# Attention scores of the grouped-query layer: four 32-row tiles of TensorE in place of a zero-padded key matrix, with the softmax's steps dealt out anew to the engines

## The chip, the cores and the metric

The kernel runs on one core of one Trainium2 chip, in float32. The time is the device time of one execution in microseconds (us); lower is better. Engines are called PE (TensorE), DVE (VectorE), ACT (ScalarE), POOL (GpSimd) and SP (SyncE).

## The reference, cut to what matters

Four layers follow one another: a cross-attention block with a mixture of experts, a second attention with a choice of the best tokens, a grouped-query transformer layer, and a last attention. The change lies in the third. Its batch is 16, its sequences are 128 long, its width is D = 256; it has 16 query heads on 4 key heads, of head size 64.

```
NH, NKV, HD = 16, 4, 64
q, k = rope(q), rope(k)              # halves of 32: x1*cos - x2*sin, x2*cos + x1*sin
scores = einsum('bhqd,bhkd->bhqk', q, k) / sqrt(HD) + attention_mask
probs  = softmax(scores)             # over the 128 keys
attn   = einsum('bhqk,bhkd->bhqd', probs, v)
```

After it come the output projection, an RMS norm and a gated MLP of width 1024.

## The kernel before

The layer runs as a loop over G = 4 groups of GB = 4 batches. Within a group every engine has one queue of instructions, written out by hand, and semaphores tie the queues together: nothing overtakes within a queue.

In each group PE first projects keys and queries, DVE multiplies them with the cosine and sine tables (L1737), and POOL adds or subtracts the products to make the rotated halves `kr` and `qr` (L1712). A partition of these holds one of 4 key heads times one of 32 places within a half. Query heads are laid out as `a` (0 to 3, the place within a key head's four) by key head `i`.

For the scores the kernel before makes `kM2`: for each key head a copy of the keys in which the rows of the other three heads are zero (ACT, 8 instructions a group, L1677). One product over all 128 rows with 512 columns then gives, for one `a`, the scores of all 4 key heads at once (L1582, two halves added up). In the trace a float32 product is two MATMUL instructions, so that such a tile of scores is 4 rows of L1582.

A "tile" n = 4*j + t here is a [128 queries, 4 heads, 128 keys] block of batch j. 16 tiles make a group. It passes through:

1. PE: scores into bank `S[n % 4]` (semaphore `scored`).
2. DVE: scale and add the mask into SBUF (L1751, `masked`), then the maximum over the keys, negated (L1756, `maxed`).
3. ACT: four exponentials of 128 columns, each with its own bias and its own accumulated sum (L457, `probs`).
4. DVE: reciprocal of the sums (L1760, `divided`).
5. POOL: multiply the tile by it (`pool_scale`, L449, `scaled`).
6. PE: turn the four [128, 128] blocks into bank `T[n % 2]` (`pe_turn`, L467, `turned`). It waits for the copy of tile n - 2.
7. ACT: copy the turned tile to SBUF (L1689, `pt_ok`), in its queue `COPY_LAG` = 5 tiles behind the exponentials: the copy of tile m stands behind the exponential of tile m + 5.
8. PE: for each batch the products with the values (L1593); ACT copies them out (L1670).

PE has each tile's scores one batch ahead of the masks: `pe.wait_ge(M["masked"], n + 1)`, then the scores of tile n + 4, then the turn of tile n - 1 (`TURN_LAG` = 1).

Of the kernel before, what the change touches and what calls it, by code (L numbers as in the profile page):

```python
# [13 lines left out]
ALU = mybir.AluOpType  # L14
# [47 lines left out]
def build(nc, A, out):  # L62
    with ExitStack() as ctx:
# [65 lines left out]
        def view(at, shape):  # L129
            n = int(np.prod(shape))  # L130
            assert at + n <= W, (at, n)
            v = reg[:, at:at + n]
            if len(shape) == 1:
                return v
            names = "abcdefgh"[:len(shape)]
            return v.rearrange(f"p ({' '.join(names)}) -> p {' '.join(names)}",
                               **{k: s for k, s in zip(names[:-1], shape)})
# [49 lines left out]
        wu2 = view(l2w + 7168, [C, FF])  # L187
        wd2 = view(l2w + 9216, [FC, D])
        qr = view(12288, [GB, 2, NT])
        kr = view(0, [2, NT])  # L190
        kM2 = view(16384, [NKV, 2, NT])
        xn2 = view(16384, [GB, D])
        V2 = view(20480, [GB, NKV, HD])
        o2T = view(0, [FC, NT])
# [215 lines left out]
        def cols_of(t, n):  # L410

            return t[:, (n // 4) % 2, 4 * (n % 4):4 * (n % 4) + 4]
# [1154 lines left out]
        with nc.Fori(0, G) as g:  # L1567
            g_next = (g + 1) & (G - 1)
            with nc.Block(no_gpsimd_drain=True) as block:
                @block.tensor  # L1570
                def _(pe):
                    J = J_l2
                    pe.wait_ge(ld["l2"], 16 * 6)
                    for h in range(2):
                        pe_project(pe, J, "k" + "AB"[h], wkv2, h * P, cT)
                    for a in range(A4):
                        for h in range(2):
                            pe_project(pe, J, f"q{a}" + "AB"[h], wq2, (2 * a + h) * P, hT)
                    def scores(j, a):

                        for h in range(2):
                            ins = nc.tensor.matmul(S[a][:, :], qr[:, a, h, j * P:(j + 1) * P],  # L1582
                                                   kM2[:, :, h, j * P:(j + 1) * P], start=(h == 0), stop=(h == 1))
                        ins.then_inc(M["scored"], 1)

                    def products(j):

                        pe.wait_ge(M["pt_ok"], 4 * j + 4)
                        for q in range(2):
                            bank = claim(pe, J, f"pv{j}_{q}")  # L1590
                            for half in range(2):
                                i = 2 * q + half
                                ins = nc.tensor.matmul(bank[half * HD:(half + 1) * HD, :], V2[:, j, i, :],  # L1593
                                                       PT[:, j % 2, i::NKV, :],
                                                       start=True, stop=True)
                            ins.then_inc(q_full[J[f"pv{j}_{q}"][0]], 1)

                    pe_values(pe, J, ["v0", "v1"], wkv2, D, cT)
                    pe.wait_ge(M["keys_ok"], 2)
                    for a in range(A4):  # L1600
                        pe.wait_ge(M["roped"], 2 * (a + 2))
                        scores(0, a)
                    for n in range(4 * GB + TURN_LAG):
                        if n + 4 < 4 * GB:
                            pe.wait_ge(M["masked"], n + 1)
                            scores(n // 4 + 1, n % 4)
                        m = n - TURN_LAG
                        if m >= 0:
                            pe_turn(pe, m)
                        if m == 4:  # L1610
                            await_read(pe, J, "v0")
                            await_read(pe, J, "v1")
                        if m % 4 == 2 and m > 4:
                            products(m // 4 - 1)
                    products(GB - 1)
                    for j in range(GB):
                        await_read(pe, J, f"pv{j}_0")
                        await_read(pe, J, f"pv{j}_1")

                    def rows_out(names, w, src):  # L1620

                        for y, name in enumerate(names):
                            bank = claim(pe, J, name)
                            for jj in range(2):
                                j = 2 * y + jj
                                for f in range(FC):
                                    ins = nc.tensor.matmul(bank[:, jj * D:(jj + 1) * D], src[:, f, j * P:(j + 1) * P],  # L1627
                                                           w[:, f, :], start=(f == 0), stop=(f == FC - 1))
                            ins.then_inc(q_full[J[name][0]], 1)

                    rows_out(["w0", "w1"], wo2, o2T)
# [12 lines left out]

                    for src, ok, names, seen in ((xn, M["xn_ok"], ["hx0", "hx1"], GB), (cn, M["cn_ok"], ["hc0", "hc1"], 0)):
                        for c in range(C):
                            bank = claim(pe, J, names[c])
                            pe.wait_ge(ok, seen + GB)
                            for j in range(GB):
                                ins = nc.tensor.transpose(bank[:, j * P:(j + 1) * P], src[:, j, c * P:(c + 1) * P], ident[:])  # L1650
                            ins.then_inc(q_full[J[names[c]][0]], 1)
                    for f in range(FC):
                        await_read(pe, J, f"u{f}")
                    rows_out(["d0", "d1"], wd2, act2)

                @block.scalar
                def _(act):
# [13 lines left out]
                                                 bank[:, :].rearrange("p (f n) -> p f n", f=4), ACT.Copy)\  # L1671
                                .then_inc(q_free[J[name][0]], 1)

                    for h in range(2):
                        act.wait_ge(M["roped"], h + 1)
                        for i in range(NKV):
                            ins = nc.scalar.activation(kM2[:, i, h, :], kr[:, h, :], ACT.Copy, scale=of_key_head[:, i:i + 1])  # L1677
                        ins.then_inc(M["keys_ok"], 1)
                    values()
                    N, LAG = 4 * GB, COPY_LAG  # L1680
                    for n in range(N + LAG):
                        if n < N:
                            act_exp(act, n, bank_of(n)[0])
                        if n >= LAG:
                            m = n - LAG
                            act.wait_ge(M["turned"], m + 1)
                            if m >= 8:
                                await_full(act, J, f"pv{m // 4 - 2}_1")
                            nc.scalar.activation(turned_tile(m), T[m % 2][:, :].rearrange("p (s q) -> p s q", q=P),  # L1689
                                                 ACT.Copy).then_inc(M["pt_ok"], 1)  # L1690

                        j = (n - 7 - LAG) // 4
                        if 0 <= j < GB - 1 and n == 4 * j + 7 + LAG:
                            out_copies(j)
                    out_copies(GB - 1)
                    for c in range(C):
# [9 lines left out]
                def _(pool):  # L1706
                    link = chained(pool, M["pchain"])
                    for r in range(1 + A4):
                        pool.wait_ge(M["multiplied"], 4 * (r + 1))
                        first, second = (kr[:, 0, :], kr[:, 1, :]) if r == 0 else (qr[:, r - 1, 0, :], qr[:, r - 1, 1, :])  # L1710
                        for dst, k1, k2, op in ((first, 0, 1, ALU.subtract), (second, 2, 3, ALU.add)):
                            nc.gpsimd.tensor_tensor(dst.rearrange("p (j n) -> p j n", j=GB), products4(k1, r),  # L1712
                                                    products4(k2, r), op).then_inc(M["roped"], 1)
                    for n in range(4 * GB):
                        pool_scale(pool, n)
                    for y in range(2):
                        rms(pool, link, 0, 2 * y + 2, slice(2 * y, 2 * y + 2))

# [4 lines left out]
                def _(dve):  # L1723
# [17 lines left out]
                            dve.sem_inc(q_free[J[n + "AB"[half]][0]], 1)  # L1741

                    dve.wait_ge(ld["mask"], 16)
                    N = 4 * GB
                    for n in range(N + 2):
                        if n < N:
                            j = n // 4
                            dve.wait_ge(M["scored"], n + 1)
                            if n >= 8:
                                dve.wait_ge(M["turned"], n - 7)  # L1750
                            nc.vector.scalar_tensor_tensor(  # L1751
# [3 lines left out]
                            dve.wait_ge(M["masked"], n + 1)  # L1755
                            nc.vector.tensor_reduce(cols_of(mx, n), bank_of(n)[0], AX, ALU.max, negate=True)\  # L1756
                                .then_inc(M["maxed"], 1)
                        if n >= 2:
                            dve.wait_ge(M["probs"], n - 1)
                            nc.vector.reciprocal(cols_of(rden, n - 2), cols_of(psum, n - 2)).then_inc(M["divided"], 1)  # L1760

                    def add_rows(names, y0=0):
                        for y, name in enumerate(names, y0):
# [120 lines left out]
```

## Time and profile before

| | |
|---|---|
| median of 3 runs | 1667.31 us (1665.19 to 1672.28) |
| the profiled execution | 1668.44 us |
| its span | 1666.6 us |
| PE busy | 1390.1 us (83%), mean granted clock 0.907 |
| DVE, ACT, POOL busy | 696.3, 623.5, 377.4 us |

The span is what the profiler saw; the execution's own time is 1.8 us longer. Lines such as L467 are lines of the kernel above; where a helper is shared by layers its rows are too. A granted clock of 1.00 is 2.4 GHz, one of 0.50 is 1.2 GHz. The attention part of a group of the third layer (from the first scores to the last output copy) takes some 47.7 us, and there are four.

### The profile page before, as it was taken

How to read it: one execution, taken by the hardware profiler on the slowest of the kernel's cores; microseconds unless marked ns; L12 is line 12 of the kernel's file. 1: busy time of each engine (PE TensorE's matmuls, PEld its weight loads, DVE VectorE, ACT ScalarE, POOL GpSimd, SP SyncE). 2: the span in 40 equal slices, each digit the busy share in tenths (PEclk: the TensorE clock that was granted, in tenths of full speed). 3: DMA queues.
4: the chain of work that ended last, by engine and by line, in shares of the span. 5: the costliest groups of instructions: out<-in, count | busy, mean ns of one | idle time of the engine just before them, and what ended most of it. 6: DMA issues, size and time to landing. Idle time of an engine off the chain costs nothing. (4 is left out here: it accounts for less than half of the span.)

```text
span 1666.6 us, 28785 instructions
## 1 busy us (share of the span) xinstructions
PE 1390.1 (83%) x11090; PEld 962.7 (58%) x11090; DVE 696.3 (42%) x1394; ACT 623.5 (37%) x1549; POOL 377.4 (23%) x473
## 2 busy tenths in 40 slices
PE   4999999655299999974666797998998899787997
PEld 2666666444299999962444345545554455554665
DVE  2677676524121000005554561262253336134666
ACT  2444444110144554431222272164237127214442
POOL 4224540022400000013331341052033124006200
PEclk9999999855599999996777799999999999998999
DMA  9900000003289999961000000000000000000000
GB/s 347 413 33 2 2 2 2 2 0 126 86 285 331 321 328 329 333 217 39 26 26 0 1 1 1 0 0 0 0 0 0 0 0 0 0 0 1 14 15 27
DMA packets 83144, 137.89 MB, mean 83 GB/s; under 512 B 5336, under 2 KB 63712, under 8 KB 83040
## 3 DMA queue, kind: packets, MB, share of 16 engines
q1 hardware_dynamic: 78672, 127.02, 21.8%
q0 software_dynamic: 3072, 8.39, 1.5%
q8 instruction: 74, 1.21, 0.3%
q10 hardware_dynamic: 1296, 1.02, 0.2%
q14 instruction: 30, 0.25, 0.0%
HBM read 107.32 MB, written 29.10 MB: 82 GB/s over the span
## 5 line engine op out<-in xcount | busy, mean ns | idle before, releaser
L369 PE MATMUL bank<-reg 128*128 128x512 f32 x416 | 192.9, 626 | 12.6 <-PEq L229 9.1
L1260 ACT ACTIVATE w_ca<-scores,fc1b 128x128 f32<-128x128 f32 x312 | 114.1, 368 | 138.5 <-PE scores L1216 118.2
L821 ACT ACTIVATE reg<-scores 128x1024 f32<-128x1024 f32 x96 | 93.1, 1021 | 161.5 <-PE scores L625 161.5
L369 PEld LDWEIGHTS bank<-reg 128*128 128x128 f32 x416 | 81.1, 201 | 120.7 <-issue 98.3
L1216 PEld LDWEIGHTS scores<-reg 128*128 128x128 f32 x1248 | 147.7, 194 | 4.6 <-issue 2.7
L1216 PE MATMUL scores<-reg 128*128 128x128 f32 x1248 | 148.1, 278 | 2.1 <-issue 1.1
L882 DVE TENSOR_REDUCE reg<-scores 128x8 f32<-128x1024 f32 x96 | 113.0, 1220 | 71.4 <-PE scores L615 71.4
L1226 PE MATMUL bank<-reg,w_ca 128*128 128x256 f32 x624 | 141.1, 379 | 0.3 <-DVE small L1273 0.3
L1226 PEld LDWEIGHTS bank<-reg,w_ca 128*128 128x128 f32 x624 | 115.6, 190 | 14.5 <-DVE small L1273 0.3
L449 POOL TENSOR_TENSOR reg<-reg,rden 128x512 f32<-128x512 f32 x80 | 83.1, 1041 | 157.7 <-DVE rden L1760 88.9
L1582 PE MATMUL scores<-reg 128*128 128x512 f32 x256 | 117.5, 594 | 0.0
L1281 DVE COPY reg<-bank 128x256 f32<-128x256 f32 x39 | 16.6, 425 | 238.5 <-PE bank L1226 238.4
L1627 PE MATMUL bank<-reg 128*128 128x256 f32 x512 | 112.4, 380 | 3.6 <-ACT reg L1670 3.5
L1627 PEld LDWEIGHTS bank<-reg 128*128 128x128 f32 x512 | 96.6, 190 | 20.7 <-issue 7.8
L457 ACT ACTIVATE reg<-reg,mx 128x128 f32<-128x128 f32 x256 | 99.7, 394 | 22.6 <-DVE mx L1756 21.3
L903 DVE RECIPROCAL reg<-bank 128x256 f32<-128x256 f32 x48 | 84.2, 1755 | 35.4 <-PE bank L640 34.5
L770 ACT ACTIVATE reg<-bank,qk_bias,shape_c 128x512 f32<-128x512 f32 x96 | 69.6, 779 | 56.6 <-PE bank L598 56.3
L467 PEld LDWEIGHTS bank<-ident,reg 128*128 128x128 f32 x320 | 40.7, 153 | 67.3 <-POOL reg L449 35.4
L467 PE MATMUL bank<-ident,reg 128*128 128x128 f32 x320 | 53.6, 299 | 28.3 <-POOL reg L449 15.6
L1297 POOL COPY pick_now<-pick_row 128x8 int32 (+1 forms) x4 | 0.8, 198 | 334.3 <-DMA expert_rows<-reg,pick_row 301.5
L1582 PEld LDWEIGHTS scores<-reg 128*128 128x128 f32 x256 | 45.5, 190 | 43.6 <-issue 43.4
L1766 DVE TENSOR_TENSOR xres<-bank,xres 128x512 f32 x16 | 11.1, 692 | 140.5 <-PE bank L1627 140.5
(236 smaller groups left out, 2251.5 us busy)
## 6 DMA issues: line engine op xcount, KB each, us to landing
reg<-in_fc SPq DMA_DIRECT2D x78, 1024.0 KB, 7.2
expert_rows<-reg SPq DMA_DIRECT2D x36, 480.0 KB, 14.6
reg<-expert_rows SPq DMA_DIRECT2D x39, 128.0 KB, 5.6
expert_rows<-reg SPq DMA_DIRECT2D x39, 128.0 KB, 6.5
xres<-in_x SPq DMA_DIRECT2D x1, 2048.0 KB, 11.6
ctxr<-in_ctx SPq DMA_DIRECT2D x1, 2048.0 KB, 8.6
w_l<-in_w_l SPq DMA_DIRECT2D x2, 1024.0 KB, 12.2
out<-xres SPq DMA_DIRECT2D x8, 256.0 KB, 2.6
```

Of the source, the lines that this page charges most:

```text
L369: ins = nc.tensor.matmul(bank[:, 0:n], w[:, c, w0:w0 + P], src[:, c, :], start=(c == 0), stop=(c == C - 1))
L449: nc.gpsimd.tensor_tensor(v, v, spread(rden, m), ALU.mult).then_inc(M["scaled"], 1)
L457: ins = nc.scalar.activation(bank_of(n)[0][:, a, :], source[:, a, :], ACT.Exp, bias=cols_of(mx, n)[:, a:a + 1], accum_out=cols_of(psum, n) ...
L467: ins = nc.tensor.transpose(T[n % 2][:, s * P:(s + 1) * P], bank_of(n)[0][:, s, :], ident[:])
L821: ins = nc.scalar.activation(PT2[:, t % 2, 2 * half:2 * half + 2, :, :, :].rearrange("p r s c q -> p (r s c q)"), scores4[:, 2 * half:2 * ...
L882: ins = nc.vector.tensor_reduce(mxpad.rearrange("p (c n d) -> p n c d", c=C, d=DH)[:, 4 * half:4 * half + 4, :, 0], scores4[:, 2 * half:2 ...
L903: link(nc.vector.reciprocal(rd, banks[4][:, 2 * P:4 * P]))
L1216: ins = nc.tensor.matmul(S[n % 4][:, 0:P], up_w8[j % 2][:, c, f * P:(f + 1) * P], xbT[:, j % 2, c, :], start=(c == 0), stop=(c == C - 1))
L1226: ins = nc.tensor.matmul(T[j % 2][:, 0:D], h1[:, j % 2, f, :], down_w8[j % 2][:, f, :], start=(f == 0), stop=(f == FC - 1))
L1260: nc.scalar.activation(h1[:, j % 2, f, :], S[n % 4][:, 0:P], ACT.Gelu, bias=fc1b[:, bass.ds(e * FC + f, 1)]).then_inc(M["fc1_free"], 1)
L1582: ins = nc.tensor.matmul(S[a][:, :], qr[:, a, h, j * P:(j + 1) * P], kM2[:, :, h, j * P:(j + 1) * P], start=(h == 0), stop=(h == 1))
L1627: ins = nc.tensor.matmul(bank[:, jj * D:(jj + 1) * D], src[:, f, j * P:(j + 1) * P], w[:, f, :], start=(f == 0), stop=(f == FC - 1))
```

## The change

- `kM2` and its 8 ACT instructions a group are gone. `kr` moves to another place in SBUF.
- The scores are computed head by head on 32 rows: for each `a`, half `h` and key head `i` a product of 32 rows by 128 columns, the four key heads after one another on the four row strips of the array and into the four banks `S[0]` to `S[3]`. A tile of DVE is now one key head with its four `a`, and all four tiles of a batch come out together: one `scored` a batch.
- PE computes the scores of batch j + 1 when all four tiles of batch j are masked, ahead of the turn of tile 4*j and behind the turn of tile 4*j - 1.
- POOL adds the negated maximum to the tile (new, `shifted`), in its queue ahead of the scaling of tile n - 2.
- ACT does one exponential of 512 columns, in place, with no bias and no sum.
- DVE sums the exponentials of tile n - 3 (a new `tensor_reduce`, which the reciprocal waits for) where it took only the reciprocal of tile n - 2.
- ACT's copies of the turned tiles stay 5 behind. The turn of tile m no longer stands one behind the scores (`TURN_LAG` isn't used here).

```diff
+                    def scores(j):
+                        at_j = slice(j * P, (j + 1) * P)
+                        for a in range(A4):
+                            if j == 0:
+                                pe.wait_ge(M["roped"], 2 * (a + 2))
+                            for h in range(2):
+                                for i in range(NKV):
+                                    r = slice(i * HALF, (i + 1) * HALF)
+                                    ins = nc.tensor.matmul(S[i][:, a * P:(a + 1) * P], qr[r, a, h, at_j], kr[r, h, at_j],
+                                                           start=(h == 0), stop=(h == 1))
                         ins.then_inc(M["scored"], 1)
...
-                    pe.wait_ge(M["keys_ok"], 2)
-                    for a in range(A4):
-                        pe.wait_ge(M["roped"], 2 * (a + 2))
-                        scores(0, a)
-                    for n in range(4 * GB + TURN_LAG):
-                        if n + 4 < 4 * GB:
-                            pe.wait_ge(M["masked"], n + 1)
-                            scores(n // 4 + 1, n % 4)
-                        m = n - TURN_LAG
-                        if m >= 0:
-                            pe_turn(pe, m)
+                    scores(0)
+                    for m in range(4 * GB):
+                        if m % 4 == 0 and m + 4 < 4 * GB:
+                            pe.wait_ge(M["masked"], m + 4)
+                            scores(m // 4 + 1)
+                        pe_turn(pe, m)
...
-                    for h in range(2):
-                        act.wait_ge(M["roped"], h + 1)
-                        for i in range(NKV):
-                            ins = nc.scalar.activation(kM2[:, i, h, :], kr[:, h, :], ACT.Copy, scale=of_key_head[:, i:i + 1])
-                        ins.then_inc(M["keys_ok"], 1)
...
-                            act_exp(act, n, bank_of(n)[0])
+                    for n in range(4 * GB + 5):
+                        if n < 4 * GB:
+                            act.wait_ge(M["shifted"], n + 1)
+                            nc.scalar.activation(bank_of(n)[0], bank_of(n)[0], ACT.Exp).then_inc(M["probs"], 1)
...
-                    for n in range(4 * GB):
-                        pool_scale(pool, n)
+                    for n in range(4 * GB + 2):
+                        if n < 4 * GB:
+                            pool.wait_ge(M["maxed"], n + 1)
+                            v = bank_of(n)[0]
+                            nc.gpsimd.tensor_tensor(v, v, spread(mx, n), ALU.add).then_inc(M["shifted"], 1)
+                        if n >= 2:
+                            pool_scale(pool, n - 2)
...
-                        if n >= 2:
-                            dve.wait_ge(M["probs"], n - 1)
-                            nc.vector.reciprocal(cols_of(rden, n - 2), cols_of(psum, n - 2)).then_inc(M["divided"], 1)
+                        if DIV_LAG <= n < N + DIV_LAG:
+                            m = n - DIV_LAG
+                            dve.wait_ge(M["probs"], m + 1)
+                            link(nc.vector.tensor_reduce(cols_of(psum, m), bank_of(m)[0], AX, ALU.add))
+                            nc.vector.reciprocal(cols_of(rden, m), cols_of(psum, m)).then_inc(M["divided"], 1)
```

Here is PE's queue in a group, between the turn of tile 2 and the turn of tile 8, as it was. The rows of L1582 are scores (one of 128x512 x2 is one tile; the first is that of tile 7), those of L467 turns of one tile, those of L1593 the products of batch 0.

```order
L467 MATMUL bank4<-ident,reg 128x128 x4
L1582 MATMUL scores4<-reg 128x512 x2
L467 MATMUL bank5<-ident,reg 128x128 x4
L1582 MATMUL scores4<-reg 128x512 x2
L467 MATMUL bank4<-ident,reg 128x128 x4
L1582 MATMUL scores4<-reg 128x512 x2
L467 MATMUL bank5<-ident,reg 128x128 x4
L1582 MATMUL scores4<-reg 128x512 x2
L467 MATMUL bank4<-ident,reg 128x128 x4
L1593 MATMUL bank6<-reg 64x512 x2
L1593 MATMUL bank7<-reg 64x512 x2
L1582 MATMUL scores4<-reg 128x512 x2
```

And now the same queue of the changed kernel, from the turn of tile 3 to the turn of tile 9. L1587 are the scores of a whole batch (here batches 2 and 3), L466 the turns, L1598 the products.

```order
L466 MATMUL bank5<-ident,reg 128x128 x4
L1587 MATMUL scores4<-reg 128x128 x32
L466 MATMUL bank4<-ident,reg 128x128 x4
L466 MATMUL bank5<-ident,reg 128x128 x4
L466 MATMUL bank4<-ident,reg 128x128 x4
L1598 MATMUL bank6<-reg 64x512 x2
L1598 MATMUL bank7<-reg 64x512 x2
L466 MATMUL bank5<-ident,reg 128x128 x4
L1587 MATMUL scores4<-reg 128x128 x32
L466 MATMUL bank4<-ident,reg 128x128 x4
L466 MATMUL bank5<-ident,reg 128x128 x4
```

Where every turn had a tile of scores ahead of it, now four turns and the products stand between one batch's scores and the next's.

The second place is POOL's queue in a group. L1706 are the last rotated halves; L1712 is the addition of the negated maximum, L448 the scaling. Before, 16 scalings stood there in one row.

```order
L1706 TENSOR_TENSOR reg<-w_ca 128x512 x2
L1712 TENSOR_TENSOR reg<-reg,mx 128x512 x3
L448 TENSOR_TENSOR reg<-reg,rden 128x512
L1712 TENSOR_TENSOR reg<-reg,mx 128x512
L448 TENSOR_TENSOR reg<-reg,rden 128x512
L1712 TENSOR_TENSOR reg<-reg,mx 128x512
```

The pairs go on to the end of the group: the addition for tile n + 1 now stands behind the scaling of tile n - 2.

## Rows read from the trace of the kernel before

**Rows 1.** Windows: one attention part; busy us and instructions of each engine, clock, DMA.
```profile
1379.20:1426.90 47.70, 43.29 (x161) 20.45 (x160) 23.58 (x48) 38.45 (x153) 17.16 (x17) 1.00 0.00 0
```

**Rows 2.** Timeline of PE: start us, us, what, idle before.
```profile
1379.19 10.46 PE L1582 MATMUL scores<-reg 128*128 128x512 f32 x24
...
1398.11 0.60 PE L467 MATMUL bank<-ident,reg 128*128 128x128 f32 x4
1398.55 1.88 PE L1582 MATMUL scores<-reg 128*128 128x512 f32 x4
1400.27 0.60 PE L467 MATMUL bank<-ident,reg 128*128 128x128 f32 x4
...
1402.95 1.94 PE L1593 MATMUL bank<-reg 128*64 128x512 f32 x8
...
1426.90 9.30 PE L1627 MATMUL bank<-reg 128*128 128x256 f32 x42 [0.89 <-ACT reg L1670]
```

**Rows 3.** Timeline of DVE, the same part: start us, us, what, idle before.
```profile
1381.30 0.69 DVE L1751 SCALAR_TENSOR_TENSOR reg<-scores,w_sa 128x512 f32<-128x512 f32 x1 [4.14 <-PE scores L1582]
...
1382.82 0.69 DVE L1751 SCALAR_TENSOR_TENSOR reg<-scores,w_sa 128x512 f32<-128x512 f32 x1
...
1389.42 0.17 DVE L1760 RECIPROCAL rden<-psum 128x4 f32<-128x4 f32 x1
1389.69 0.69 DVE L1751 SCALAR_TENSOR_TENSOR reg<-scores,w_sa 128x512 f32<-128x512 f32 x1
1390.41 0.69 DVE L1756 TENSOR_REDUCE mx<-reg 128x4 f32<-128x512 f32 x1
1391.02 0.17 DVE L1760 RECIPROCAL rden<-psum 128x4 f32<-128x4 f32 x1
...
1413.31 0.69 DVE L1751 SCALAR_TENSOR_TENSOR reg<-scores,w_sa 128x512 f32<-128x512 f32 x1 [0.66 <-PE scores L1582]
```

**Rows 4.** Waits in that part: us in total, times, longest.
```profile
DVE reg L1751 <- PE scores L1582: 13.7, 14, 4.1
```

**Rows 5.** Groups of instructions by form on ACT: busy us, mean ns, idle before.
```profile
L457 ACT ACTIVATE reg<-reg,mx 128x128 f32<-128x128 f32 x256 | 99.7, 394 | 22.6 <-DVE mx L1756 21.3
L457 ACT ACTIVATION_READ_ACCUMULATOR reg<-reg,mx 128x1 f32 x256 | 48.9, 191 | 0.0
L1689 ACT ACTIVATE reg<-bank 128x512 f32<-128x512 f32 x64 | 36.6, 588 | 8.7 <-PE bank L467 8.7
L1677 ACT ACTIVATE reg<-reg,shape_c 128x512 f32<-128x512 f32 x32 | 20.1, 711 | 24.2 <-POOL reg L1712 24.2
```

**Rows 6.** The same on POOL.
```profile
L449 POOL TENSOR_TENSOR reg<-reg,rden 128x512 f32<-128x512 f32 x80 | 83.1, 1041 | 157.7 <-DVE rden L1760 88.9 <-DVE rden L430 68.8
L1712 POOL TENSOR_TENSOR reg<-w_l 128x512 f32<-128x512 f32 x16 | 20.1, 1275 | 7.7 <-DVE w_l L1737 7.7
```

**Rows 7.** The last layer, 32-row tiles: a window, then PE's timeline.
```profile
1635.00:1640.00 5.00, 4.72 (x84) 3.38 (x84) 2.77 (x4) 0.22 (x1) 0.00 (x0) 0.66 0.00 0
...
1636.38 1.88 PE L635 MATMUL bank<-reg 128*32 128x128 f32 x32
...
1643.13 1.17 PE L615 MATMUL scores<-reg 32*128 32x128 f32 x32
1644.23 1.08 PE L635 MATMUL bank<-reg 128*32 128x128 f32 x32
```

**Rows 8.** A wait of PE and the clock around it: timeline row, then windows.
```profile
1445.03 1.57 PE L1637 MATMUL bank<-ident,reg 128*128 128x128 f32 x6 [3.86 <-DVE reg L1530]
...
1422.00:1426.00 4.00, 2.73 (x14) 0.99 (x12) 0.00 (x0) 2.17 (x4) 0.00 (x0) 1.00 0.00 0
1442.00:1446.00 4.00, 0.97 (x5) 0.85 (x6) 1.55 (x6) 0.22 (x1) 1.29 (x4) 0.92 0.00 0
1446.00:1450.00 4.00, 3.18 (x6) 1.37 (x5) 0.00 (x0) 2.44 (x3) 0.00 (x0) 0.50 0.00 0
1450.00:1454.00 4.00, 4.00 (x8) 1.77 (x7) 0.43 (x1) 0.60 (x1) 0.00 (x0) 0.73 0.00 0
```

More of the change, by code:

```diff
@@ L189, in build @@
         qr = view(12288, [GB, 2, NT])
-        kr = view(0, [2, NT])
-        kM2 = view(16384, [NKV, 2, NT])
+        kr = view(16384, [2, NT])
         xn2 = view(16384, [GB, D])
@@ L1578, in _ @@
                             pe_project(pe, J, f"q{a}" + "AB"[h], wq2, (2 * a + h) * P, hT)
-                    def scores(j, a):
-                        for h in range(2):
-                            ins = nc.tensor.matmul(S[a][:, :], qr[:, a, h, j * P:(j + 1) * P],
-                                                   kM2[:, :, h, j * P:(j + 1) * P], start=(h == 0), stop=(h == 1))
+                    def scores(j):
[8 more added lines that the diff above has]
+                                                           start=(h == 0), stop=(h == 1))
                         ins.then_inc(M["scored"], 1)
@@ L1593, in products @@
                                 ins = nc.tensor.matmul(bank[half * HD:(half + 1) * HD, :], V2[:, j, i, :],
-                                                       PT[:, j % 2, i::NKV, :],
+                                                       PT[:, j % 2, A4 * i:A4 * (i + 1), :],
                                                        start=True, stop=True)
@@ L1672, in out_copies @@
                                 .then_inc(q_free[J[name][0]], 1)
-                    for h in range(2):
-                        act.wait_ge(M["roped"], h + 1)
-                        for i in range(NKV):
-                            ins = nc.scalar.activation(kM2[:, i, h, :], kr[:, h, :], ACT.Copy, scale=of_key_head[:, i:i + 1])
-                        ins.then_inc(M["keys_ok"], 1)
-                    values()
-                    N, LAG = 4 * GB, COPY_LAG
-                    for n in range(N + LAG):
-                        if n < N:
-                            act_exp(act, n, bank_of(n)[0])
-                        if n >= LAG:
-                            m = n - LAG
+                    values()
+                    for n in range(4 * GB + 5):
+                        if n < 4 * GB:
+                            act.wait_ge(M["shifted"], n + 1)
+                            nc.scalar.activation(bank_of(n)[0], bank_of(n)[0], ACT.Exp).then_inc(M["probs"], 1)
+                        if n >= 5:
+                            m = n - 5
                             act.wait_ge(M["turned"], m + 1)
@@ L1690, in _ @@
                                                  ACT.Copy).then_inc(M["pt_ok"], 1)
-                        j = (n - 7 - LAG) // 4
-                        if 0 <= j < GB - 1 and n == 4 * j + 7 + LAG:
+                        j = (n - 12) // 4
+                        if 0 <= j < GB - 1 and n == 4 * j + 12:
                             out_copies(j)
@@ L1743, in _ @@
                     dve.wait_ge(ld["mask"], 16)
-                    N = 4 * GB
-                    for n in range(N + 2):
+                    N, DIV_LAG = 4 * GB, 3
+                    for n in range(N + DIV_LAG):
                         if n < N:
                             j = n // 4
-                            dve.wait_ge(M["scored"], n + 1)
+                            dve.wait_ge(M["scored"], j + 1)
                             if n >= 8:
```

## The prediction

> **What bounds the kernel now.** Only the attention part of the third layer's four groups changes, so I looked at how long such a part is and who is late in it. The windows view gives PE 43.29 of 47.70 us busy at a clock of 1.00, ACT 38.45, DVE 23.58, POOL 17.16 [rows 1]. PE's timeline shows why: a turn starts at 1398.11, scores at 1398.55, the next turn at 1400.27, with no idle between, so each tile costs PE 0.44 + 1.72 = 2.16 us, and the products about 1.9 us once a batch [rows 2]. The waits say the same from the other side: DVE waited 14 times, 13.7 us, for scores, and of nothing else for long [rows 4]. ACT is full too: four exponentials of 0.39 us and a copy of 0.59 make 2.15 us a tile [rows 5]. So the part is bound by PE, with ACT level with it and DVE (0.72 + 0.61 + 0.27 = 1.60 us a tile, [rows 3]) well below. Its frame: scores start at 1379.19, the first mask at 1381.30, the last mask at 1413.31, and PE begins the next step at 1426.90 [rows 2, 3]. From first to last mask 32.0 us, then a tail of 13.6 us.
>
> **What each edit costs by itself.**
>
> *Scores.* The last layer runs 32-row tiles of this shape: 32 instructions start at 1643.13 and the next piece at 1644.23, 1.10 us [rows 7]. A batch has 4 x 2 x 4 products of two instructions, 64, so 2.20 us against 4 x 1.72 = 6.88. PE loses 18.7 us of work a group. The key copies on ACT (8 x 0.71 us, [rows 5]) ended before PE wanted them and free nothing.
>
> *Exponential.* One of 512 columns on ACT: not in the trace. Above, the key copy, SBUF to SBUF with a scale from memory, 0.71; below, 0.59 for a copy out of PSUM [rows 5]. I take 0.60. ACT falls to 1.2 us a tile.
>
> *Shift.* One more tensor operation on POOL. With a broadcast operand 1.04 us, with two full ones 1.27 [rows 6]; this one is of the first kind, only ADD for MULT. I take 1.04: POOL is at 2.08 of each tile. At 1.27 it would add about 0.7 us a group.
>
> *Sum.* DVE gets a reduction of 0.69 us, which the reciprocal waits for, 0.03 more. A tile on DVE: mask 0.72, maximum 0.61, sum 0.72, reciprocal and step 0.27, together 2.32 us [rows 3]. This alone is more than PE's 2.16 was. The first three tiles have no sum and take 1.52 (1381.30 to 1382.82).
>
> **What the new order makes late.** The scores of batch j + 1 are no longer behind a mask alone. They stand behind the turn of tile 4j - 1; that turn waits for the copy of tile 4j - 3; ACT has this copy behind the exponential of tile 4j + 2; that waits for the shift of tile 4j + 2, which POOL has behind the scaling of tile 4j - 1; and this waits for DVE's reciprocal of tile 4j - 1, which is the last thing DVE does in its step 4j + 2. So from the end of that step: scaling 1.04, shift 1.04, exponential 0.60, copy 0.59, turn 0.44, scores 2.20, and six handovers of some 0.05, together 6.2 us, and 0.23 more until the first mask of a batch (scores from 1379.19, 1.88 us long, mask at 1381.30). Meanwhile DVE has one step, 2.32 us. It stands still for 4.1 us at batches 2 and 3.
>
> A group, in us after its first mask: mask 3 starts at 3 x 1.52 = 4.56 and ends at 5.25; scores of batch 1, for which no turn stands in the way, 2.20 + 0.28, mask 4 at 7.75. Mask 8 at 7.75 + 4 x 2.32 + 4.1 = 21.1; mask 12 at 34.5; mask 15 at 34.5 + 6.96 = 41.5, against 32.0. First mask: 0.4 later than before, as the whole batch must be there (2.20 + 0.28 for 2.11).
>
> The tail: DVE's step 15 ends at +2.3, scaling 12 and shift 15 at +4.5, exponential 15 at +5.1. ACT then has two copies, the two output copies of batch 1 and copy 12, 5 x 0.55, +7.9; turn 14 and the products of batch 2, +10.2; turn 15, its copy and one output copy, +11.9; the last products and their copy, +14.4. Before 13.6.
>
> Sum at full clock: 0.4 + 9.5 + 0.8 = 10.7 us a group, 43 us for four. The profiled execution took 1668.4, so 1711.
>
> **The clock.** Before, PE was never long idle here: even at 2.73 us busy of 4 the clock stayed at 1.00 [rows 8]. Now PE has 8.8 us of scores, 7 of turns and 7.5 of products in some 58 us, 40%, and in long gaps: none between the first scores and mask 3 (over 5 us), then four turns of 0.44 in some 10 us, and so again after each batch's scores. The nearest rows: after 3.86 us idle (0.97 of 4 busy) the clock is 0.50 in the next window and back only within 1450 to 1454, after PE has worked almost without a gap since 1445.03 [rows 8]. In the last layer, after short gaps, the same piece of 32 instructions takes 1.88 us for 1.08, in a window of clock 0.66 [rows 7]. So each burst of a batch starts at 1.2 GHz, and a burst is on the path. Scores 1 wholly: 2.2 us more. Turn 3 with scores 2: 2.6. [...] In the tail, some 1.0. Together 7.8 a group, 31 us for four: 1742. The bounds are nothing (the level stays at 2.4 GHz: 1711), and every piece of PE on that path at 1.2 GHz (three scores 6.6, three turns 1.3, three products 5.6: 13.5 a group, 1765).
>
> [...]
>
> **The rivals.**
> 1. *The stalls without the clock*, 1711. For it: 2.73 of 4 us busy kept 1.00. Against: the gaps here are longer than the one of 3.86 us that did not.
> 2. *The clock stays down throughout*, 1765. For it: bursts of 5 us are hardly longer than what brought it back. Against: it did come back.
> 3. *DVE never waits for scores*: not slower. It decides if the chain of 6.2 us fits into DVE's 2.32, that is if PE can issue the scores long before the turn ahead of them is let go. Then the last mask is at 4.56 + 12 x 2.32 = 32.4, the group costs 0.4 + 0.4 + 0.8 = 1.6 us more, the kernel 1674, within half a per cent. For it: PE's and ACT's own work falls far below 2.3 us a tile. Against: queues don't overtake, and the order shows the turn there. It would be faster than before only if the tail shrank too.
> 4. *The row tiles don't overlap*, as pairs now add up in one bank: at the 0.11 us of a full-array instruction (0.44 for 4, [rows 2]) 64 take 7.0 us, 4.8 more at each of four places, 1711 + 77 = 1788. Against: [rows 7], where four strips write four banks in just this order.
>
> [...]
>
> **How the numbers follow.** Chances: stalls and a clock that falls and returns 0.68; rival 1 0.15; rival 2 0.09; rival 3 0.06, of which 0.02 for a shorter tail and so faster; rival 4 0.02. The time is that of the first, less 1 us because the profiled execution was 1.1 above the median: 1741. The range goes to just under rival 1 and over rival 2 with the slower shift (0.7 x 4 = 3 us) and exponential: 1706 to 1770. It leaves out rivals 3 and 4 and the far ends. Half a per cent, 8 us, is about what a measurement can tell from no change. Faster 0.02, same 0.05, slower 0.93.
>
> **What would show it.** DVE's mask of tiles 8 and 12 waits over 4 us for PE, that of tile 4 about 1 at full clock and 3 at half; DVE's step is 2.32 us, POOL's shift 1.04, the exponential 0.60; the copies on ACT wait for nothing in the middle of a group while turns wait for copies; scores take 2.2 us where the clock is 1.00 and up to 4.4 where it is 0.50; an attention part is 58 us long at full clock, 66 with the clock's losses. I am wrong if DVE's waits for scores sum to under 5 us a group (rival 3), or if the clock in the attention part is above 0.95 (rival 1). What the rows can't tell is whether POOL and DVE slow each other once both work on SBUF nearly all the time; DVE's step would then be longer than 2.32 us.

## The result, and the profile after

The changed kernel takes 1725.4 us (median; 1724.9 to 1727.0), the kernel before beside it 1668.6. The ratio is 1.034, 95% interval 1.032 to 1.037: slower by 3.4%, where 1741 us was forecast with a range of 1706 to 1770. The profiled execution took 1724.9 us, its span is 1723.1.

The windows view of the last group's attention part, and of pieces of it (columns as in [rows 1]):

```profile
1421.50:1485.00 63.50, 35.48 (x353) 22.48 (x353) 33.23 (x64) 22.90 (x41) 33.07 (x33) 0.73 0.00 0
1424.00:1428.00 4.00, 0.00 (x0) 0.00 (x0) 3.90 (x7) 0.87 (x2) 2.07 (x2) 0.82 0.00 0
1443.40:1447.20 3.80, 3.80 (x66) 3.57 (x66) 0.00 (x0) 0.95 (x2) 0.00 (x0) 0.52 0.00 0
1460.80:1462.80 2.00, 2.00 (x66) 1.88 (x65) 0.00 (x0) 0.00 (x0) 0.00 (x0) 1.00 0.00 0
```

The part is 63.5 us long where it was 47.7 [rows 1]. No engine is busy for more than 56% of it, and the mean clock is 0.73 where it was 1.00. In the second row PE does nothing and the clock falls, from 1.00 in its first two us to 0.80 in the third and 0.50 in the fourth; the third and fourth rows are the scores of batches 2 and 3. The four parts of the run are 63.3, 63.5, 63.5 and 63.5 us, 62.6 us more together; between them the run is some 6 us shorter, which leaves the 56.5 us by which the spans differ. No run explains these 6 us.

PE's timeline of that part (start, us, what, idle before):

```profile
1421.55 2.07 PE L1587 MATMUL scores<-reg 32*128 32x128 f32 x64
1428.58 3.80 PE L1587 MATMUL scores<-reg 32*128 32x128 f32 x64 [4.96 <-DVE reg L1750]
...
1440.29 1.09 PE L466 MATMUL bank<-ident,reg 128*128 128x128 f32 x4 [3.68 <-ACT reg L1684]
1442.39 1.09 PE L466 MATMUL bank<-ident,reg 128*128 128x128 f32 x4 [1.01 <-ACT reg L1684]
1443.41 3.79 PE L1587 MATMUL scores<-reg 32*128 32x128 f32 x64
...
1455.14 1.09 PE L466 MATMUL bank<-ident,reg 128*128 128x128 f32 x4 [1.03 <-ACT reg L1684]
1456.16 3.68 PE L1598 MATMUL bank<-reg 128*64 128x512 f32 x8
1459.77 1.10 PE L466 MATMUL bank<-ident,reg 128*128 128x128 f32 x4
1460.80 2.07 PE L1587 MATMUL scores<-reg 32*128 32x128 f32 x64
...
1485.01 14.05 PE L1627 MATMUL bank<-reg 128*128 128x256 f32 x64 [0.89 <-ACT reg L1670]
```

The reader sees both halves of the loss. A batch's scores take 2.07 us at a clock of 1.00 (batches 0 and 3) and 3.80 at 0.50 (batch 1, 1428.60 to 1432.40), where the four tiles of before took 6.9 us: PE's work did fall. But its work now comes in bursts, with a copy of ACT (L1684) or a mask of DVE (L1750) ahead of most of them. DVE's timeline around the scores of batches 2 and 3:

```profile
1438.81 0.18 DVE L1761 RECIPROCAL rden<-psum 128x4 f32<-128x4 f32 x1
1438.90 0.66 DVE L1750 SCALAR_TENSOR_TENSOR reg<-scores,w_sa 128x512 f32<-128x512 f32 x1
1439.60 0.69 DVE L1755 TENSOR_REDUCE mx<-reg 128x4 f32<-128x512 f32 x1
1440.20 0.68 DVE L1760 TENSOR_REDUCE psum<-reg 128x4 f32<-128x512 f32 x1
1440.91 0.18 DVE L1761 RECIPROCAL rden<-psum 128x4 f32<-128x4 f32 x1
1447.40 0.69 DVE L1750 SCALAR_TENSOR_TENSOR reg<-scores,w_sa 128x512 f32<-128x512 f32 x1 [6.30 <-PE scores L1587]
...
1463.06 0.69 DVE L1750 SCALAR_TENSOR_TENSOR reg<-scores,w_sa 128x512 f32<-128x512 f32 x1 [7.09 <-PE scores L1587]
```

The chain into the first of these waits can be read off POOL's and ACT's timelines: scaling of tile 3 (its reciprocal, the first row above, ended at 1438.99), shift of tile 6, exponential of tile 6, copy of tile 1; then PE's turn of tile 3 at 1442.39 and the scores at 1443.41.

```profile
1439.07 1.04 POOL L448 TENSOR_TENSOR reg<-reg,rden 128x512 f32<-128x512 f32 x1
1440.07 1.04 POOL L1712 TENSOR_TENSOR reg<-reg,mx 128x512 f32<-128x512 f32 x1
...
1441.14 0.63 ACT L1678 ACTIVATE reg<-reg 128x512 f32<-128x512 f32 x1 [0.99 <-POOL reg L1712]
1441.67 0.58 ACT L1684 ACTIVATE reg<-bank 128x512 f32<-128x512 f32 x1
...
1456.53 0.58 ACT L1684 ACTIVATE reg<-bank 128x512 f32<-128x512 f32 x1
```

From 1438.99 to the mask at 1447.40 it is 8.4 us. Turn and scores ran at clocks of 0.50 and 0.52 and took 0.46 and 1.72 us more than at 1.00 (1.09 for 0.63, 3.79 for 2.07); without that the chain is 6.2 us, where 6.4 was reckoned. Into the scores of batch 3 another way ended last. The turn of tile 7 had its copy (that of tile 5, the last row above) at 1457.11, but PE came to it only at 1459.77: from the turn of tile 6 at 1455.14 on it worked without a pause through that turn, the products of batch 0 and the turn of tile 7, at a clock of 0.50 up to 1460.40 and 0.59 from there to 1460.80.

The waits over this part, and the new operations' rows by form (busy us, mean ns, idle before):

```profile
DVE reg L1750 <- PE scores L1587: 20.4, 4, 7.1
PE bank L466 <- ACT reg L1684: 18.4, 8, 5.2
```

```profile
L1712 POOL TENSOR_TENSOR reg<-reg,mx 128x512 f32<-128x512 f32 x64 | 66.4, 1038 | 15.8 <-DVE mx L1755 15.8
L1760 DVE TENSOR_REDUCE psum<-reg 128x4 f32<-128x512 f32 x64 | 43.2, 675 | 4.9 <-ACT reg L1678 4.9
L1678 ACT ACTIVATE reg<-reg 128x512 f32<-128x512 f32 x64 | 40.3, 630 | 144.9 <-POOL reg L1712 144.8
```

### The profile page after: what moved, and what is told of

Its sections match the earlier page's. It is cut to its first block and busy times, and to the rows that moved or that the text cites. A ratio compares the mean times of both kernels' runs of the same rounds, so it can differ in the third digit from the quotient of the medians.

```text
span 1723.1 us, 29933 instructions
## 1 busy us (share of the span) xinstructions
PE 1354.3 (79%) x11858; PEld 969.1 (56%) x11858; DVE 734.8 (43%) x1458; ACT 540.9 (31%) x1069; POOL 440.3 (26%) x537
## 5 line engine op out<-in xcount | busy, mean ns | idle before, releaser
L368 PE MATMUL bank<-reg 128*128 128x512 f32 x416 | 186.9, 610 | 12.5 <-PEq L228 9.2
L466 PE MATMUL bank<-ident,reg 128*128 128x128 f32 x320 | 69.3, 362 | 103.0 <-ACT reg L1684 73.6
L1215 PEld LDWEIGHTS scores<-reg 128*128 128x128 f32 x1248 | 147.7, 194 | 4.6 <-issue 2.6
L466 PEld LDWEIGHTS bank<-ident,reg 128*128 128x128 f32 x320 | 46.9, 182 | 135.6 <-POOL reg L448 97.8
L448 POOL TENSOR_TENSOR reg<-reg,rden 128x512 f32<-128x512 f32 x80 | 82.8, 1039 | 141.6 <-DVE rden L1761 70.0
L1678 ACT ACTIVATE reg<-reg 128x512 f32<-128x512 f32 x64 | 40.3, 630 | 144.9 <-POOL reg L1712 144.8
L1750 DVE SCALAR_TENSOR_TENSOR reg<-scores,w_sa 128x512 f32<-128x512 f32 x64 | 43.4, 678 | 81.3 <-PE scores L1587 81.3
L1712 POOL TENSOR_TENSOR reg<-reg,mx 128x512 f32<-128x512 f32 x64 | 66.4, 1038 | 15.8 <-DVE mx L1755 15.8
```

Source lines behind the costliest of these rows:

```text
L368: ins = nc.tensor.matmul(bank[:, 0:n], w[:, c, w0:w0 + P], src[:, c, :], start=(c == 0), stop=(c == C - 1))
L448: nc.gpsimd.tensor_tensor(v, v, spread(rden, m), ALU.mult).then_inc(M["scaled"], 1)
L466: ins = nc.tensor.transpose(T[n % 2][:, s * P:(s + 1) * P], bank_of(n)[0][:, s, :], ident[:])
L1215: ins = nc.tensor.matmul(S[n % 4][:, 0:P], up_w8[j % 2][:, c, f * P:(f + 1) * P], xbT[:, j % 2, c, :], start=(c == 0), stop=(c == C - 1))
L1712: nc.gpsimd.tensor_tensor(v, v, spread(mx, n), ALU.add).then_inc(M["shifted"], 1)
```

## The experiments

Part below is the length of the third group's attention part, from the first scores to PE's first instruction behind the last output copy: 47.7 us before, 63.5 after. The four parts of a run agree within 0.5 us, but for three runs: row tiles with early scores and filler (47.6 to 48.7), softmax with copies 3 behind (its first part is 48.0) and mixed with filler (44.9 to 46.3, mean 45.6). Each ratio is to the kernel before as measured beside that run: 1668.6 us for the first row, 1668.2 for the next four, 1670.9 for the four behind them, 1667.0 for the last three.

| kernel | part, us | time, us | ratio to before [95%] |
|---|---|---|---|
| after | 63.5 | 1725.4 | 1.034 [1.032, 1.037] |
| row tiles only | 56.7 | 1702.9 | 1.021 [1.016, 1.025] |
| softmax only | 57.8 | 1704.8 | 1.020 [1.014, 1.026] |
| after, copies 3 behind | 56.5 | 1698.3 | 1.018 [1.013, 1.023] |
| after, filler on PE | 59.8 | 1709.4 | 1.024 [1.019, 1.029] |
| after, scores two turns earlier | 54.2 | 1700.7 | 1.017 [1.013, 1.020] |
| row tiles only, scores earlier | 49.4 | 1676.2 | 1.002 [1.001, 1.004] |
| the same with filler | 47.6 | 1671.7 | 1.000 [0.998, 1.002] |
| softmax only, copies 3 behind | 49.2 | 1673.4 | 1.001 [0.999, 1.003] |
| mixed softmax | 46.2 | 1661.5 | 0.996 [0.995, 0.998] |
| mixed softmax with filler | 44.9 | 1659.9 | 0.995 [0.994, 0.997] |
| before, copies 4 behind | 46.5 | 1657.8 | 0.995 [0.994, 0.997] |

### Row tiles without the new softmax

The diff is cut: POOL only scales again, and DVE's reciprocal is again 2 tiles behind.

```diff
-                            act.wait_ge(M["shifted"], n + 1)
-                            nc.scalar.activation(bank_of(n)[0], bank_of(n)[0], ACT.Exp).then_inc(M["probs"], 1)
+                            act_exp(act, n, bank_of(n)[0])
...
-                            nc.gpsimd.tensor_tensor(v, v, spread(mx, n), ALU.add).then_inc(M["shifted"], 1)
...
-                            link(nc.vector.tensor_reduce(cols_of(psum, m), bank_of(m)[0], AX, ALU.add))
```

> The changed kernel with the old softmax: ACT does four exponentials of 128 columns with bias and sum (1.57 us a tile) and the copies 5 behind, DVE takes only the reciprocal, POOL only scales; the scores come from row tiles, a batch at a time, in the changed kernel's PE order. Queue theory with the clock: a turn still stands behind a copy, behind an exponential three tiles on, and the batch's scores behind the turn, and PE has long gaps, so an attention part takes 57 to 59 us and the kernel about 1705 to 1712; DVE waits for scores 3 to 6 us at each batch and the clock of the part is 0.7 to 0.85. Rival (the extra operations on DVE and POOL are what costs): with them gone the time falls to 1669 to 1680 and the part to about 49 us.

1702.9 us, part 56.7. Time and part are just below what was expected, and far from the rival's: with DVE and POOL back at their old work, 60% of the slowdown is still there. DVE's longest wait for scores is 7.3 us, where at most 6 was expected, even without a shift in the chain, as the exponentials in it take 1.57 us (four of 0.39) and not 0.63.

### The new softmax without the row tiles

The kernel before with the changed kernel's code on POOL, ACT and DVE; its scores and their order on PE are untouched.

> The kernel before with its zero-padded key product and its PE order, one tile of scores ahead of each turn, but the new softmax: POOL adds the maximum, one exponential, DVE sums three tiles later. Queue theory: scores of tile n + 4 wait for a turn that waits for a copy behind an exponential behind a shift, so PE is no longer gapless, but it stalls a little at each tile and not at each batch, and the clock mostly stays: part 54 to 58 us, kernel 1692 to 1710. Rival (extra work is what costs): all of the 57 us of the change appear here, 1720 to 1727. Rival (only the row tiles cost): 1668 to 1675.

1704.8 us, part 57.8, as the queue theory said, and neither rival's. So each half alone costs about 2%, and the two are not simply added. Both have the same late link: over the four groups turns wait for copies for 63.1 us with the row tiles alone, 31.1 with the softmax alone, 73.6 in the changed kernel.

### The copies nearer to their turns

```diff
-                        if n >= 5:
-                            m = n - 5
+                        if n >= 3:
+                            m = n - 3
```

(and the output copies with them, still behind the copy of tile 4j + 7).

> The changed kernel with ACT's copy of a turned tile 3 exponentials behind, not 5. A turn then waits for the exponential of the next tile alone, which is long done, and the chain into a batch's scores loses the shift, the exponential and the copy, 2.2 us, at batches 2 and 3. Queue theory with the clock: part 58 to 60.5 us, kernel 1706 to 1716, as PE still has its gaps and stays at 1.2 GHz in them; at full clock it would be 1682. If the copies' place in ACT's queue doesn't matter: 1725.

1698.3 us, 27 us less than the changed kernel and more than was expected of it. In this run's waits the turns wait for copies for 5.0 us in all; in the changed kernel it was 73.6. Part of that wait has only moved: the turns now wait for POOL's scaling, 54.0 us in all, where it was 10.2 us in the changed kernel.

```profile
PE bank L466 <- POOL reg L448: 54.0, 32, 3.2
...
PE bank L466 <- ACT reg L1684: 5.0, 4, 1.3
```

DVE's mask of a new batch still waits, 3.58 us in the piece below, since the turn ahead of the scores waits for POOL's scaling; the scores start only at 1420.44, as DVE's step ends, and take 3.3 us, at a clock of 0.61.

```profile
1423.90 0.69 DVE L1750 SCALAR_TENSOR_TENSOR reg<-scores,w_sa 128x512 f32<-128x512 f32 x1 [3.58 <-PE scores L1587]
```

### Work for PE in its gaps

```diff
+                    def fill(bank, n):
+                        for _ in range(n):
+                            nc.tensor.matmul(bank[:, :], ident[:], wq2[:, 0, 0:512], start=True, stop=True)
                     scores(0)
+                    fill(T[0], 6)
...
                         if m == 4:
                             await_read(pe, J, "v0")
                             await_read(pe, J, "v1")
+                            fill(claim(pe, J, "pv0_0"), 6)
```

> The changed kernel with 6 products of 128 by 512 columns (5 us) that nobody reads, put on PE in the gap between the scores of batches 0 and 1, and 6 more in the gap behind the turn of tile 4. They write banks that are free and delay nothing if the gaps are 5 us long. Clock theory: scores 1 then run at 2.4 GHz (2.07 us where they took 3.80), as do the products, turns and scores before batch 3: part 59 to 60 us, kernel 1710 to 1716. If the clock isn't a cause but only the queues: 1725 or a little more. If the filler itself delays PE: over 1728.

1709.4 us, part 59.8, as expected: 16 us less by giving PE more to do. PE's timeline of its last group, L1607 being the filler:

```profile
1409.11 2.07 PE L1587 MATMUL scores<-reg 32*128 32x128 f32 x64
1411.11 5.42 PE L1607 MATMUL bank<-reg,ident 128*128 128x512 f32 x12
1416.46 2.07 PE L1587 MATMUL scores<-reg 32*128 32x128 f32 x64
1418.79 0.66 PE L466 MATMUL bank<-ident,reg 128*128 128x128 f32 x4 [0.27 <-POOL reg L448]
1422.10 1.12 PE L466 MATMUL bank<-ident,reg 128*128 128x128 f32 x4 [2.66 <-POOL reg L448]
```

The scores of batch 1 take 2.07 us, at a clock of 1.00, for 3.80. Some 3.5 us later, with one turn done in the meantime, the clock is down again: the turn at 1422.10 takes 1.12, at 0.50. The scores of batch 2, with no filler ahead of them, take 3.80 us, at 0.50; behind the second filler the products take 1.94 us and the scores of batch 3 take 2.07, both at 1.00. This shows that the clock is a cause of its own, and that here the filler in one gap did nothing for the burst behind the next.

### The scores two turns earlier

```diff
-                        if m % 4 == 0 and m + 4 < 4 * GB:
-                            pe.wait_ge(M["masked"], m + 4)
-                            scores(m // 4 + 1)
+                        if m == 0 or (m % 4 == 2 and m + 6 < 4 * GB):
+                            j = (m + 2) // 4
+                            pe.wait_ge(M["masked"], 4 * j + 4)
+                            scores(j + 1)
                         pe_turn(pe, m)
```

> The changed kernel with one place in PE's queue moved: the scores of batch j + 1 stand ahead of the turn of tile 4j - 2 and its products, two turns earlier than before; each waits as it did for the four masks of batch j. Queue theory: DVE then waits for scores only some 1.2 us at full clock instead of 6 to 7 us at batches 2 and 3, but scores now come out of a gap of PE and run at 1.2 GHz each time: 3.8 us, so a wait of 3 to 4 us at each batch; part 56 to 57 us, kernel 1698 to 1706. Rival (DVE's and POOL's longer steps set the pace, not the queue): 1720 or more.

1700.7 us, part 54.2; the time is as expected, the part 2 us shorter. Moving one line of PE's queue takes back 25 of the 57 us, or nearly 30 by the ratios. And it shows what is left: the scores come straight behind a wait of PE and run at a clock of 0.50 to 0.52, at all three batches.

```profile
1407.91 3.79 PE L1587 MATMUL scores<-reg 32*128 32x128 f32 x64 [4.96 <-DVE reg L1751]
...
1418.94 3.72 PE L1587 MATMUL scores<-reg 32*128 32x128 f32 x64 [2.84 <-DVE reg L1751]
...
1428.49 0.63 PE L466 MATMUL bank<-ident,reg 128*128 128x128 f32 x4 [3.83 <-ACT reg L1685]
1429.97 3.80 PE L1587 MATMUL scores<-reg 32*128 32x128 f32 x64 [0.85 <-DVE reg L1751]
```

The last of them started after a gap of only 0.85 us; what stood ahead of it was one turn in 5.3 us (1428.49, behind 3.83 us of idleness), and that turn still took 0.63 us, at a clock of 1.00. The length of the gap just ahead doesn't tell the level: 1.00 behind 3.83 us, 0.50 behind 0.85.

### Row tiles, old softmax, early scores; then with filler

The first and the fifth edit together; then with 4 products behind the first scores.

> Row tiles with the old softmax and the scores of a batch two turns earlier (both edits of the two runs before together). ACT at 2.15 us a tile is the slowest engine; at full clock the part would be 46.3 us, under the kernel before. Clock theory: PE works 1.4 us of each 2.15, the scores run at 1.2 GHz part of the time: part 50 to 52 us, kernel 1676 to 1686. If the clock did not matter: 1661.

> The same with 4 products of 128 by 512 columns that nobody reads (3.7 us) between the scores of batches 0 and 1. Clock theory: scores 1 run at 2.4 GHz, 1.7 us a group less than the same kernel without the filler: part 48.5 to 50 us, kernel 1670 to 1678. If the clock isn't what the gap costs: the same time as without the filler.

1676.2 us, part 49.4; with filler 1671.7, parts 47.6 to 48.7. Where the scores stand early, row tiles cost 0.2%, an interval that just leaves out 1; with filler nothing is left that a measurement tells. They don't gain either. ACT's exponentials and copies come 2.02 us apart where nothing holds them, little under the 2.16 of before, and without filler ACT still waits 6.0 us a part for the maxima, behind scores of 3.80 and 3.55 us (clocks of 0.50 and 0.55) at batches 1 and 2.

### The new softmax with near copies

The softmax-only kernel with the copies 3 behind (`N, LAG = 4 * GB, 3`).

> The key product and PE order of before, the new softmax on POOL, ACT and DVE, and ACT's copies 3 behind. Queue theory: with the copy no longer behind a late exponential PE runs without a gap again and the extra operations on DVE (2.10 us a tile) and POOL (2.08) just fit under PE's 2.16: part 48 to 50 us, kernel 1668 to 1676. Rival (the extra work itself costs): as with the softmax alone at 5 behind, 1700 or more.

1673.4 us, part 49.2, against 57.8 with the copies 5 behind: one number takes away nearly the whole cost. The part is still 1.5 us longer than before; in the time no difference can be told, 1.001 [0.999, 1.003]. PE's rhythm is that of [rows 2] again, scores from 1396.01 to the next at 1398.16, 2.15 us, and DVE keeps up, 2.13 us from mask to mask:

```profile
1396.01 1.88 PE L1582 MATMUL scores<-reg 128*128 128x512 f32 x4
1397.72 0.60 PE L467 MATMUL bank<-ident,reg 128*128 128x128 f32 x4
1398.16 1.88 PE L1582 MATMUL scores<-reg 128*128 128x512 f32 x4
...
1396.37 0.69 DVE L1757 SCALAR_TENSOR_TENSOR reg<-scores,w_sa 128x512 f32<-128x512 f32 x1
...
1398.50 0.68 DVE L1757 SCALAR_TENSOR_TENSOR reg<-scores,w_sa 128x512 f32<-128x512 f32 x1
```

So the extra operations as such, 0.68 us on DVE and 1.04 on POOL for each tile, cost next to nothing in a good order.

### Towards a faster version

With neither DVE (2.10) nor ACT (2.15) leaving room under 2.16, a mix: three tiles of a batch as before, the fourth with shift, one exponential and sum.

```diff
+                            if n % 4 == 3:
+                                act.wait_ge(M["shifted"], n // 4 + 1)
+                                nc.scalar.activation(bank_of(n)[0], bank_of(n)[0], ACT.Exp).then_inc(M["probs"], 1)
+                            else:
+                                act_exp(act, n, bank_of(n)[0])
```

It has the changed kernel's row tiles and PE order, copies 3 behind, reciprocals 2 behind and POOL's additions and scalings one tile closer together; the second run adds 4 filler products. The third run is the kernel before with nothing changed but its copies, 4 behind in place of 5.

> Row tiles in the changed kernel's PE order, copies 3 behind, reciprocals 2 behind, and the two softmaxes mixed: three tiles of a batch with four exponentials with bias and sum on ACT, the fourth with POOL's shift, one exponential and DVE's sum. Per tile ACT has 1.9 us, DVE 1.8, POOL 1.3, PE 1.4. By the queues at full clock the part would be 43.6 us and the kernel 1650; by the clock theory PE's gaps bring 1.2 GHz and take 5 us back: part 49 us, kernel 1670 to 1676. If the clock costs nothing here: 1650 to 1655.

> The same with 4 products of 128 by 512 columns that nobody reads (3.7 us) behind the first scores. Clock theory: part 47 to 48 us, kernel 1662 to 1670, level with the kernel before or a little faster.

> The kernel before with ACT's copies of the turned tiles in the third layer 4 behind instead of 5. PE's pace in the middle is the same 2.16 us a tile; at the end of a group one exponential less stands ahead of the late copies, so the tail is some 1 us shorter: kernel 1662 to 1668. If the tail doesn't hang on ACT's queue: no change, 1668.

1661.5, 1659.9 and 1657.8 us; all three are faster than the kernel before, by 0.4, 0.5 and 0.5%. All three came out lower than expected. The mixed kernels did so though the scores of batches 1 and 2 took 3.80 us, at a clock of 0.50, in the first of them as feared: I had charged the clock 5 us here, and against the 43.6 us reckoned at full clock it took some 2.6 (an estimate). In the third the part is 46.5 us with the clock at 1.00 throughout:

```profile
1369.05:1415.50 46.45, 43.05 (x161) 20.54 (x160) 23.48 (x48) 38.13 (x153) 17.09 (x17) 1.00 0.00 0
```

Its tail is shorter, from the last mask at 1403.17 to 1415.52, 12.4 us for 13.6: 1.2 us a group, 5 us in all. The time fell by 9. The rest isn't explained by the edit; stretches that it doesn't touch differ by some us from execution to execution (the first part starts at 956.23 here, at 962.91 in the profile of before).

The mixed kernels have their copies nearer too, 3 behind, and one number in the kernel before gains as much as they do. So no run shows that the row tiles or the mixed softmax have a share in their gain. Nor was the whole change run with both repairs, early scores and near copies, together.

## Why the prediction was right, point by point

*What bounds it before.* Right in the main: PE at 2.16 us a tile. ACT was a little lower than the 2.15 that I had, which adds up durations that overlap; its tiles come 2.04 us apart where nothing holds them (from 1397.72 to 1399.76 in the kernel before). Relief for one of the two moved nothing for the better (row tiles with early scores 1.002, softmax with near copies 1.001).

*The prices.* Scores 2.07 us for 2.20, shift 1.04 for 1.04, exponential 0.63 for 0.60, sum 0.68 for 0.69: right. The price that was mis-sized is DVE's step: 2.10 to 2.13 us where I had 2.32, and 1.32 where I had 1.52 for the first three. I had read 0.27 us from the start of a reciprocal to the next mask; it is 0.09, the rest was a wait that the row I took didn't show. Nine of the long steps and three of the short ones lie on the path, so that is 2.4 us a group, 10 in all, of the 16 by which the forecast was too high. Some 6 more are the stretches outside the parts, which came out shorter than before and which the sum had as unchanged.

*The chain into a batch's scores.* At batch 2 right in every link: scaling, shift, exponential, copy, turn, scores, 6.2 us at full clock for 6.4. At batch 3 the copy of tile 5 wasn't the last to come, the work of PE from the turn of tile 6 on was; at full clock the two ways would be some 0.3 us apart (an estimate: turn and products 0.44 + 1.87 us from 1455.14, against the copy's end at 1457.11), so the sum was no worse for it. Taking out the copy's place in it (copies 3 behind) gave 27 us back, moving the scores ahead of it 25. DVE's waits are 2.5 us at batch 1, 6.3 at batch 2 and 7.1 at batch 3, where I had some 3, 6.7 and 6.1.

*The clock.* Right that it falls, and where: scores 1 and 2 took 3.80 and 3.79 us at clocks of 0.50 and 0.52, scores 3 took 2.07 us at 1.00, with the dense work ahead of them.

```profile
1428.60:1432.40 3.80, 3.80 (x65) 3.58 (x66) 1.42 (x3) 0.82 (x2) 2.48 (x3) 0.50 0.00 0
1455.10:1460.40 5.30, 5.26 (x15) 2.12 (x16) 0.83 (x3) 2.23 (x4) 2.90 (x3) 0.50 0.00 0
1460.40:1460.80 0.40, 0.40 (x3) 0.08 (x1) 0.00 (x0) 0.00 (x0) 0.00 (x0) 0.59 0.00 0
```

At batch 3 the price lies in the work ahead: two turns of 1.09 us and products of 3.68 for 1.94. Of the 7.8 us charged a group, 2.0 stood for turn 6, the products, turn 7 and scores 3; no run shows this term, it was an estimate of mine. What the run shows there is PE at work without a pause from 1455.14 and the clock at 1.00 only from about 1460.8 on, nearly 6 us later, which by the rows costs some 2.9 us. Behind the wait of [rows 8] it was 4.6 us of work without a gap at a clock of 0.50, from 1447.42, before the clock rose (0.91 in the window behind):

```profile
1447.40:1452.00 4.60, 4.58 (x6) 2.02 (x7) 0.00 (x0) 1.82 (x2) 0.00 (x0) 0.50 0.00 0
1452.00:1453.00 1.00, 1.00 (x4) 0.49 (x3) 0.00 (x0) 0.00 (x0) 0.00 (x0) 0.91 0.00 0
```

Rival 1, the stalls alone, with the steps and the chain as measured: first mask at 2.3 us, mask 4 at 7.0 after it, masks 8 and 12 each 12.5 later (three steps of 2.11 and the chain), mask 15 at 38.3, a tail of some 14, together 55 us for what is 63.5. The difference, 8.5 us a group, is near the 7.8 that I charged, and the filler's 16 us show that it is real. Part of this is luck: by the rows the first two terms are 1.7 us for 2.2 and 2.3 for 2.6, the third some 2.9 for 2.0, and the tail 1.6 for 1.0, so that too much here made up for too little there. That all of it is the clock was not shown, as no run with row tiles kept the clock at 1.00 throughout.

That each burst of a batch starts at half the clock is borne out for the long bursts: the turns at 1440.29, 1453.02 and 1468.68, behind waits of 3.68 to 5.22 us, take 1.09 us, each at a clock of 0.50. It isn't for each turn that stands alone: one at 1435.96, behind 2.53 us, took 0.66 us, and the one behind 3.83 us in the kernel with early scores 0.63, both at 1.00.

*The first mask and the tail.* First mask 1423.88, 2.3 us after the scores' start, for 2.5. From the last mask (1469.43) to the end 15.6 us, for 14.4 and 1.0 for the clock: right.

*Rivals.* 2, the clock down throughout: not so, scores 3 took 2.07 us at a clock of 1.00, behind nearly 6 us of work. 3, DVE never waits: not so in this order. It waited 20.4 us a part for scores, and what held it up was the order of the queues. The kernels with early scores (1676) and with near copies (1673) come close to its 1674, but each has only half of the change, so that this bears on it and doesn't show it. 4, tiles that don't overlap: 64 instructions took 2.07 us where 7.0 were reckoned without overlap, so they do.

## What to carry to other kernels

When work is lumped (a batch's scores at once where there was a tile at a time), read for the lump's place in its queue what the instruction ahead of it waits for, link by link, before adding up anybody's busy time. A distance such as "copies 5 behind" is tuned to how early the exponential is; when a new step makes the exponential later, a shorter distance should be tried. Here that one number was worth 27 and 31 us in two kernels and 9 in the kernel before, where neither new idea gained anything that was shown. And count on losing a part of the time saved on TensorE where the saving opens gaps: here the scores of batches 1 and 2 saved 3.1 us each and not 4.8, as they ran at clocks of 0.50 and 0.52, and so did turns (1.09 us for 0.63) and products (3.68 for 1.94) ahead of batch 3.

## What was not expected of the hardware

More work on TensorE made the kernel faster: 12 products a group that nobody reads, 11 us of PE time, took 16 us off the run. In the kernel with early scores the clock was 0.50 behind a gap of 0.85 us (scores 3.80 us), when the 5.3 us before held only one turn, while at the end of a group of the changed kernel turns and products with gaps of 0.34 to 0.84 us between them ran at 1.00 (turns of 0.63 us). As reckoned, but worth knowing, POOL's addition of a broadcast operand costs 1.04 us for 512 columns, as its multiplication does, where the same with two full operands costs 1.27 [rows 6].
